# Normalisers of the first 512 rows of each batch in a linear attention: inverted whole and spread by transfers instead of products

## What is computed

```
q = elu(x @ Wq.T) + 1          # feature map, per head
k = elu(x @ Wk.T) + 1
v = x @ Wv.T
kv = einsum('bhtd,bhte->bhde', k, v)
z = 1.0 / (einsum('bhtd,bhd->bht', q, k.sum(axis=2)) + 1e-06)
out = einsum('bhtd,bhde,bht->bhte', q, kv, z)
x = layernorm(x + out @ Wo.T)
```

## Time and profile before

| | before |
|---|---|
| timed runs, median of 3 | 909.43 us (909.2 to 910.33) |
| profiled execution, first to last instruction (span) | 907.6 us |
| PE busy | 886.1 us, 98% |
| DVE busy | 617.3 us, 68% |
| ACT busy | 401.0 us, 44% |
| POOL busy | 343.9 us, 38% |
| TensorE clock granted, mean | 0.995 of full |

### The profile page before, as it was taken

The page is one execution under the profiler, slowest core; times in us unless marked ns, Lnnn a source line. Parts: engine busy times, 40 slices in busy tenths (PEclk is TensorE's granted clock), DMA queues, the critical chain, the costliest instruction groups (busy, mean ns, idle before and its releaser), DMA issues.

```text
span 907.6 us, 13733 instructions
## 1 busy us (share of the span) xinstructions
PE 886.1 (98%) x4946; PEld 715.0 (79%) x4946; DVE 617.3 (68%) x1171; ACT 401.0 (44%) x661; POOL 343.9 (38%) x334
## 2 busy tenths in 40 slices
PE   8999999999999999999999999999999999999994
PEld 7777877876888888888768877888878878888883
DVE  5755754487987798798679837765788786544513
ACT  5544333544444634643564546353532454322222
POOL 3000400004877434344234473625349223733441
PEclk9999999999999999999999999999999999999998
DMA  9632021203110000000010200010200543232311
GB/s 290 181 113 93 11 73 58 83 13 101 40 36 1 0 1 1 1 1 0 1 47 1 100 7 1 2 46 2 94 24 13 205 143 94 71 117 93 142 44 47
DMA packets 43975, 54.21 MB, mean 60 GB/s; under 512 B 6114, under 2 KB 25859, under 8 KB 43907
## 3 DMA queue, kind: packets, MB, share of 16 engines
q1 hardware_dynamic: 42082, 49.11, 16.9%
q0 software_dynamic: 1824, 4.22, 1.4%
HBM read 42.78 MB, written 10.52 MB: 59 GB/s over the span
## 4 chain that ended last, share of the span: by engine, by line
PE 67%; DVE 5%; issue 2%; ACT 2%; POOL 0%; DVEq 0%; ACTq 0%
PE ps L41 15%; PE ps L43 15%; PE ps L42 15%; PE ps L2393 8%; PE ps L2394 8%; DVE acc L1757 2%; PE ps L2533 2%; PE ps L2439 1%; PE ps L2540 1%; PE ps L2516 1%; PE ps L2505 1%; PE ps L2674 0%; PE ps L2620 0%; PE ps L2472 0%; DVE xsel L2009 0%
## 5 line engine op out<-in xcount | busy, mean ns | idle before, releaser
L1757 DVE SCALAR_TENSOR_TENSOR acc<-ps,gu_scale,acc 128x512 f32<-128x512 f32 x264 | 197.5, 749 | 48.2 <-ACT acc L1455 28.4
L2393 PE MATMUL ps<-xt_hi,gu_val 128*128 128x512 f32 x352 | 140.5, 399 | 3.2 <-PEq L71 1.5
L2394 PE MATMUL ps<-xt_lo,gu_val 128*128 128x512 f32 x352 | 137.2, 390 | 0.0
L1455 ACT ACTIVATE acc<-ps,gu_scale 128x512 f32<-128x512 f32 x88 | 60.6, 689 | 89.4 <-PE ps L2394 89.3
L2292 POOL TENSOR_TENSOR fsg<-fsg,acc 128x512 f32<-128x512 f32 x44 | 58.9, 1339 | 108.8 <-DVE acc L1757 104.8
L2393 PEld LDWEIGHTS ps<-xt_hi,gu_val 128*128 128x128 f32 x352 | 66.0, 187 | 28.2 <-DVE acc L1757 11.2
L2394 PEld LDWEIGHTS ps<-xt_lo,gu_val 128*128 128x128 f32 x352 | 66.1, 188 | 12.1
L2297 POOL TENSOR_TENSOR fh_lo<-fsg,fh_hi 128x512 fp32r<-128x512 f32 x44 | 59.0, 1340 | 42.7 <-ACT fh_hi L1467 42.7
L2358 POOL TENSOR_TENSOR mh_lo<-mh,mh_hi 128x512 fp32r<-128x512 f32 x31 | 41.2, 1328 | 72.8 <-ACT mh_hi L1686 72.7
L41 PE MATMUL ps<-dn_hi,fh_hi 128*128 128x512 f32 x172 | 67.6, 393 | 0.0
L42 PE MATMUL ps<-dn_hi,fh_lo 128*128 128x512 f32 x172 | 67.1, 390 | 0.0
(11 more groups left out here) (323 smaller groups left out, 2113.2 us busy)
## 6 DMA issues: line engine op xcount, KB each, us to landing
mw_raw<-in_w SPq DMA_DIRECT2D x16, 512.0 KB, 3.8
a_nib<-in_gate_up_packed SPq DMA_DIRECT2D x88, 64.0 KB, 2.6
x<-x SPq DMA_DIRECT2D x16, 256.0 KB, 2.9
mw_raw<-x SPq DMA_DIRECT2D x8, 512.0 KB, 4.3
out<-mw_raw SPq DMA_DIRECT2D x8, 512.0 KB, 3.0
xt_raw<-in_xT SPq DMA_DIRECT2D x3, 1024.0 KB, 4.9
x<-in_x SPq DMA_DIRECT2D x3, 1024.0 KB, 5.3
a_nib<-in_down_packed SPq DMA_DIRECT2D x8, 256.0 KB, 3.4
```

The lines of the kernel that those rows point to most:

```text
L1455: act.activation(acc[part][u // 2 % 2][:, :], ps[:, FG, :], ACT.Copy, scale=gu_scale[:, part * IT + j, 0:1]).then_inc(s_g0, 1)
L1757: dve.scalar_tensor_tensor(out=a[:, :], in0=ps[:, FG + c, :], scalar=gu_scale[:, part * IT + j, c:c + 1], in1=a[:, :], op0=ALU.mult, op1=A ...
L2393: pe.matmul(ps[:, FG + c, :], gu_val[:, o, c, :], xt_hi[b % 2][:, c, :], start=True, stop=False)
L2394: pe.matmul(ps[:, FG + c, :], gu_val[:, o, c, :], xt_lo[b % 2][:, c, :], start=False, stop=True).then_inc(s_gu, 1)
```

## The change

For half 0 of each batch only:

- `first_normalisers(b)` takes the place of `normalisers(b, 0)`: 4 matmuls of 32 output rows and 512 columns, one for each channel group, into the whole bank `ps[:, SMALL, :]`. It no longer stands behind query(b,1,0) but inside it, after its sixth matmul of twelve.
- `inverse(b, 0)` now works on 128x512 elements (a new tile `first_inv`), and stands ahead of queries(b,1,0) on DVE instead of behind it. It also waits for `s_v`, the unpacked weights.
- `spread(b, 0)` and its 16 matmuls are gone. Instead POOL's `spread_first(b)` waits for the inverse and issues four transfers from SBUF to SBUF, one for each g: each copies four partitions of `first_inv` (512 floats, 2 KB each) to 32 partitions each, 128 rows of 2 KB or 256 KB in all, into a new tile `z`, which lies where `q_hi[b][0]` is written later. Each has its own semaphore.
- `normalised(b, 0, g)` waits for transfer g and reads `z` in SBUF instead of the PSUM bank.
- `spread_first(0)` stands ahead of the `xt_lo` subtraction on POOL, `spread_first(1)` ahead of batch 1's layer-norm steps.

Half 1 keeps its 16 + 16 small matmuls; `spread(b)` now waits for the merged low parts instead of q.

```diff
+        first_inv = put("a_first_inv", [P, BLK], 192)
+        z = [put(f"a_z{b}", [P, KC, BLK], q_hi_at[b][0]) for b in range(NB)]
...
             def inverse(b, h):
                 dve.wait_ge(s_z, 2 * b + h + 1)
-                dve.wait_ge(s_bc, 2 * b + h)
-                done(dve.tensor_scalar(inv[b][:, :], ps[:, SMALL, 0:P], 1e-6, None, ALU.add))
-                dve.reciprocal(inv[b][:, :], inv[b][:, :]).then_inc(s_zi, 1)
+                if h == 0:
+                    out, sums = first_inv[:, :], ps[:, SMALL, :]
+                    dve.wait_ge(s_v, NCHUNK if b else LATE_CHUNK)
+                else:
+                    out, sums = inv[b][:, :], ps[:, SMALL, 0:P]
+                done(dve.tensor_scalar(out, sums, 1e-6, None, ALU.add))
+                dve.reciprocal(out, out).then_inc(s_zi, 1)
...
             def normalised(b, h, g):
-                dve.wait_ge(s_bc, 2 * b + h + 1)
-                dve.tensor_tensor(q[b][h][:, g, :], ps[:, GROUP + g, :], q[b][h][:, g, :], ALU.mult).then_inc(s_qs, 1)
+                if h == 0:
+                    dve.wait_ge(s_fbc[g], 16 * (b + 1))
+                    spread_inverse = z[b][:, g, :]
+                else:
+                    dve.wait_ge(s_bc, b + 1)
+                    spread_inverse = ps[:, GROUP + g, :]
+                dve.tensor_tensor(q[b][h][:, g, :], spread_inverse, q[b][h][:, g, :], ALU.mult).then_inc(s_qs, 1)
...
                 merged_low(b, 3)
+                inverse(b, 0)
                 queries(b, 1, 0)
-                inverse(b, 0)
...
+            def spread_first(b):
+
+                pool.wait_ge(s_zi, 2 * b + 1)
+                for g in range(KC):
+                    pool.dma_start(z[b][:, g, :], first_inv[g * DH:g * DH + HG, :].unsqueeze(1).to_broadcast([HG, DH, BLK])).then_inc(s_fbc[g], 16)
...
+                    if between and c == 1:
+                        first_normalisers(b)
...
+            def first_normalisers(b):
                 pe.wait_ge(s_ks, b + 1)
-                pe.wait_ge(s_qr, 2 * KC * b + KC * (h + 1))
-                if h == 0:
-                    pe.wait_ge(s_kvl, b + 1)
-                else:
-                    pe.wait_ge(s_zi, 2 * b + 1)
+                pe.wait_ge(s_qr, 2 * KC * b + KC)
+                pe.wait_ge(s_kvl, b + 1)
+                for g in range(KC):
+                    ins = pe.matmul(ps[g * DH:(g + 1) * DH, SMALL, :], k_sum[b][:, g, PAD:PAD + DH], q[b][0][:, g, :], start=True, stop=True,
+                                    skip_group_check=True)
+                ins.then_inc(s_z, 1)
...
-                query(b, 1, 0)
-                normalisers(b, 0)
+                query(b, 1, 0, True)
                 if b:
                     transpose_rows(0)
                 query(b, 1, 1)
-                spread(b, 0)
```

More of the change, by code:

```diff
@@ L206, in linear_attention @@
                                                 for i, name in enumerate(("all", "hi", "lo")))
+        XTH_THIRD = 3
         SLOTS_A = 6
@@ L281, in linear_attention @@
         s_bc = sem("a_normaliser_spread")
+        s_fbc = [sem(f"a_first_normaliser_spread{g}") for g in range(KC)]
         s_qs = sem("a_q_normalised")
@@ L721, in _ @@
                                    pattern=[[-SEL, TB], [-1, HG], [0, DH]], channel_multiplier=1).then_inc(s_sel, 1)
-            pool.wait_ge(s_xth, 3)
+            def spread_first(b):
+                pool.wait_ge(s_zi, 2 * b + 1)
+                for g in range(KC):
+                    pool.dma_start(z[b][:, g, :], first_inv[g * DH:g * DH + HG, :].unsqueeze(1).to_broadcast([HG, DH, BLK])).then_inc(s_fbc[g], 16)
+            spread_first(0)
+            pool.wait_ge(s_xth, XTH_THIRD)
             pool.tensor_tensor(xt_lo[0][:, :, :], xt_raw[0][:, :, :], xt_hi[0][:, :, :].bitcast(F32), ALU.subtract).then_inc(s_x2l, 1)
@@ L727, in _ @@
                     pool.memset(k_sum[1][:, :, :], 0.0).then_inc(s_zero, 1)
+                    spread_first(1)
                 pool.wait_ge(s_var, i + 1)
@@ L783, in add_kv, with query @@
                 ins.then_inc(s_kvt, 1)
-            def query(b, h, m):
+            def query(b, h, m, between=False):
                 i = 2 * KC * b + KC * h + m
@@ L810, in merge, with normalisers @@
                                True, True).then_inc(s_m, 1)
-            def normalisers(b, h):
+            def first_normalisers(b):
                 pe.wait_ge(s_ks, b + 1)
-                pe.wait_ge(s_qr, 2 * KC * b + KC * (h + 1))
-                if h == 0:
-                    pe.wait_ge(s_kvl, b + 1)
-                else:
-                    pe.wait_ge(s_zi, 2 * b + 1)
+                pe.wait_ge(s_qr, 2 * KC * b + KC)
[4 more added lines that the diff above has]
+                ins.then_inc(s_z, 1)
+            def normalisers(b):
+                pe.wait_ge(s_qr, 2 * KC * b + 2 * KC)
+                pe.wait_ge(s_zi, 2 * b + 1)
                 for t in range(TB):
@@ L821, in normalisers, with spread @@
                         ins = pe.matmul(ps[g * DH:(g + 1) * DH, SMALL, 0:P], k_sum[b][:, g, PAD - SEL * t:PAD - SEL * t + DH],
-                                        q[b][h][:, g, t * P:(t + 1) * P], start=(t == 0), stop=(t == TB - 1), skip_group_check=True)
+                                        q[b][1][:, g, t * P:(t + 1) * P], start=(t == 0), stop=(t == TB - 1), skip_group_check=True)
                 ins.then_inc(s_z, 1)
-            def spread(b, h):
+            def spread(b):
                 pe.wait_ge(s_sel, KC + 1)
[L827 to L831, removed]
+                pe.wait_ge(s_zi, 2 * b + 2)
+                pe.wait_ge(s_ml, KC * (b + 1))
                 for t in range(TB):
@@ L906, in _ @@
                 project_out(b, 0)
-                normalisers(b, 1)
+                normalisers(b)
                 project_out(b, 1)
-                spread(b, 1)
+                spread(b)
                 for t in range(2, NT):
```

## The result

| | before | after |
|---|---|---|
| timed runs, median of 4 | 909.85 us (909.2 to 910.33) | 952.42 us (950.0 to 953.5) |
| ratio to before, 95% interval | | 1.0468 (1.0457 to 1.048) |
| span of the profiled execution | 907.6 us | 951.7 us |
| granted clock, mean | 0.995 | 0.971 |

The changed kernel is 4.7% slower, and outside the forecast range. The page of after shows the two places, one in each batch: PE falls to 4 and 6 tenths in one pair of slices and to 6 and 5 in a second pair, and the granted clock dips in the same parts of the span (the earlier trace rows for before).

What follows compares the result with a forecast made beforehand. The prediction took PE, busy for 98% of the span, to bound the kernel. 909.43 + 1.4 us (batch 0) + 0.95 us (batch 1) gave 911.8 us; the range for 8 in 10 was 909.6 to 945.

Steps and rivals of the forecast that it cites:

- the nearest row: POOL's transfer at the kernel's end, also 128 rows of 2 KB: 2.8 us from issue to landing, taken for the new transfers.
- the third group: First output tile of project_out, batch 0: PE's longest new wait stands before it, going on at 87.7 instead of 86.35.
- The source is the bound: Rival on the transfers: four source partitions give out one packet at a time, so landings come late; 934 us and more, chance 0.25.
- the unshared figure: Each transfer's four partitions serve it alone: landing 13.8 us after issue, 934 us with the four side by side.
- the rival's own sum: Late landings carried through to the total: 13.8 us after issue makes +12.4 and +12.0 us in the two batches, 934 us.
- The inverse: On DVE ahead of queries(b,1,0), over 512 columns: reciprocal 3.35 us, in all 4.07 us instead of 1.28.
- The four products: On PE inside query(b,1,0), 512 columns each in place of sixteen of 128: next matmul 1.01 us behind their start, upper bound 3.5.
- POOL's issues: Four transfers issued by POOL 1.33 us apart, landing in batch 0 at 80.64, 81.94, 83.24 and 84.54.
- the chain: Normalised, query_high, query_exp, queries, normalised on DVE and ACT, ending PE's waits: +1.4 us in batch 0, +0.95 in batch 1.
- the prediction's own sign: The chain is wrong if PE reaches batch 0's second normalisers at another time than 89.7 although landings are as forecast.
- Four queues for each transfer: Rival on the transfers: packets go to four of 16 queues, each lands 2.2 us later; 916 us, chance 0.14.
- the waits behind the selection products belong to DVE and ACT: PE's waits in project_out at 86.35 and 88.33 end a DVE and ACT chain; removing products takes 1.30 us off PE's list.

Runs made afterwards that it cites:

- e2_wide: Changed kernel, but each POOL transfer reads all 128 partitions of first_inv once instead of four partitions 32 times: 911.95 us, ratio to before 1.0026.
- e4_four_places: Changed kernel, but the four transfers read the partitions from 0, 8, 16 and 24, four each: 932.89 us, ratio to before 1.0259.
- e12_by_64: Changed kernel, but the four transfers read the partitions from 0, 64, 8 and 72, four each: 933.56 us, ratio to before 1.0264.
- e10_filled_long: Changed kernel with 18 and 20 filler products of 512 columns on PE while it waits for the transfers: 950.66 us, ratio to before 1.0464.
- e6_products: Changed kernel with four selection products of 512 columns on PE in place of the transfers: 909.08 us, ratio to before 0.9999.
- e1_sp: Changed kernel with the same four transfers issued by SP through the hardware queues instead of by POOL: 981.2 us, ratio to before 1.079.
- e8_order: Kernel before with one exchange on ACT, query_exp(b,1,2) ahead of query_high 2 instead of behind it: 907.45 us, ratio to before 0.9982.
- e3_one_place: Changed kernel, but all four transfers read partitions 0 to 3: 988.92 us, ratio to before 1.0875.
- e7_filled: Changed kernel with 76 and 80 filler products of 128 columns on PE while it waits for the transfers: 954.41 us, ratio to before 1.0495.
- e5_apart: Changed kernel with a group's four heads on every eighth of its 32 rows, so each transfer reads partitions eight apart: 924.35 us, ratio to before 1.0164.

## Why the prediction was wrong

**The step that failed is the landing of the transfers.** I took 2.8 us from "the nearest row", a transfer of equal size whose source spreads over 128 partitions. The size was not what decided. e2_wide shows that 2.8 us is right for a wide source, and the change's own source gave 21.3. With it the path moved too: with the landing of 2.8 us the longest wait of PE in batch 0 is before the third group, as I said (1.55 us in e2_wide), with 21.3 us it is before the first group, 17.94 us.

**The rival that came true was priced too low.** "The source is the bound" had its mechanism right, that four partitions give out their data slowly. Its landing of 13.8 us and its 934 held each transfer's four partitions to be a place of their own. Where that is so, the runs agree: 12.9 us and 932.89 (e4_four_places), 12.7 us and 933.56 (e12_by_64). In the change partitions 0 and 32 share a place, as do 64 and 96. My sentence on the Trainium skill (SBUF — State Buffer, "Door 1: The DMA port swizzle") said so, yet I put the sum on the unshared figure and gave the whole case 0.25.

**The range ended too low even by the port's rate.** The prediction's estimate from the Trainium skill's 27.6 GB/s was 9.5 us for 256 KB. With two transfers at one place the landing is then estimated at 2.8 - 0.7 + 2 x 9.5 = 21.1 us, measured 21.3. Carried through the rival's own sum (13.8 us made +12.4 and +12.0) this gives +19.7 and +19.3, so 948.4 and not the 945 that I wrote: a slip. On `normalised` 0 of batch 0 the runs show 99.39 instead of 79.89, 20.0 us with the 0.49. The rest up to 952 is about what the half clock, which I named and left unpriced, costs in after's own profile, 4.1 us against e10_filled_long. The timed medians don't show it, so this part stays open.

**What held, and what didn't, besides:**
- The inverse: 3.35 us for the reciprocal, as forecast from two shorter ones; the addition 0.69 (forecast 0.68).
- The four products: the next matmul comes 0.99 us behind their start (73.07 against 72.08; forecast 1.01), in a timeline that runs 0.5 us early; PE's wait before query(0,1,2) 0.53 us (forecast 0.7).
- Not POOL's issues: four took 3.02 us, about 0.76 each, where I had put the transfers 1.3 us apart. The real pace is quicker than I took it.
- The total, had the landings been 2.8 us: e2_wide takes 911.95 us, I had 911.8. That is luck in part, for its parts agree less well. Against before, e2_wide, whose timeline runs 0.24 us early, is 0.5 us late at the second normalisers of batch 0 (88.81 against 88.33; I had 1.4), 1.6 us at those of batch 1 (192.86 against 191.25, so +1.1; I had 0.95), and 2.4 at the first product of the next stage. These last 0.8 us I had not foreseen, and they make up for the chain's smaller loss. By the prediction's own sign the chain was thus mis-sized: 88.81 and not 89.7, and the quicker issues fit that, with `normalised` 2 at 82.39 instead of 83.24. PE at that product in before and in e2_wide:

```profile
214.37 0.47 PE L2393 MATMUL ps<-xt_hi,gu_val 128*128 128x512 f32 x1 [1.45 <-PEq L71]
```

```profile
216.79 0.77 PE L2417 MATMUL ps<-xt_hi,gu_val 128*128 128x512 f32 x1 [2.26 <-PEq L71]
```

  The wait is that of PE's sequencer, and it is as long in after. e6_products, without transfers, has 1.59, and e1_sp, where SP issues them, 1.58. So it goes with POOL's issues; why was not tried.
- Four queues for each transfer: true (e1_sp), but POOL's transfers go to different ones, so that it didn't bind.
- That the waits behind the selection products belong to DVE and ACT: e8_order gains 1.6 us and keeps the products. That removing the products saves nothing by itself is argued, not shown: no run takes them out without transfers in their place.

## What to carry to other kernels

Before a product is replaced by a transfer, count the partitions that the transfer reads, not only its bytes, and those 32 apart as one place: a broadcast from four partitions pays for every copy at the source. And before work is taken off the engine that is busy 98% of the time, look for the waits behind it: here they belonged to DVE and ACT, and exchanging two steps on ACT, which cost nothing, gave the 0.2% that this change could not.

## What the runs showed of the hardware

- Reading SBUF by transfers is bound by the place of the source. The median landing of POOL's 256 KB transfers was 39.9, 21.3, 12.9, 7.8 and 2.8 us with one, two, four, eight and all places for the four together. From 39.9 to 21.3, half a MB less at the busiest place, it is 28 GB/s; from 21.3 to 12.9, a quarter of a MB less, 31 GB/s; from 12.9 to 7.8, 26 GB/s.
- Slow transfers hold up others. SP's load of `xt_raw` (1 MB), issued in the same stretch, landed after 4.9 us before, 22.0 in after and 38.7 in e3_one_place, where POOL's transfers are the slow ones. In e1_sp it took 34.4, but there it stands behind them in SP's own list.
- PE stood 7.21 us among 76 short fillers in batch 0 of e7_filled while the queues were full, and not at all with a quarter as many. But among the 80 of its batch 1, with the queues at 83%, it didn't stand either, so this happened once. That the instructions themselves came late is my guess; no run shows it.
- After a wait PE may come back at half clock: in after behind 17.94 us of it, in e5_apart behind 4.72, in e2_wide behind the 2.26 shown above, where 512 columns then go every 0.43 us instead of 0.23 for 3.4 us. The same wait, 2.27 us, left it at full clock in e3_one_place and e4_four_places, so the wait alone doesn't decide it. Work that PE does in such a stretch goes at half the pace, so there a wait can cost more than its length. Between the landings of after, the half clock lasted on through waits of 0.58 and 1.49 us.
